# A graph layer on one core: adjacency tiles loaded one by one, or in pairs

## The reference

```python
h = jnp.maximum(_layernorm(x, axis=-1), 0.0)          # x: 10000 x 128
# _L0_gnn_ref(user_feat=h, item_feat, adj, ...)
h = item_feat @ W_item.T + b_item                      # 10000 x 128
b = user_feat @ W_user.T + b_user                      # 10000 x 128
return jax.nn.relu(adj @ h + b)                        # adj: 10000 x 10000, fp32
# result
x = x + ...
```

## Time and profile before

| | |
|---|---|
| median of three runs | 1099.3 us |
| profiled execution, time / span | 1099.52 / 1097.7 us |
| PE busy | 1090.9 us, 99% of the span |
| DVE busy | 969.6 us, 88% |
| ACT busy | 758.9 us, 69% |
| DMA | 421.56 MB, 384 GB/s over the span, the DMA engines 90% busy or more in 39 of 40 slices |
| TensorE's granted clock | full speed in all 40 slices |
| tile loads, from issue to landing | median 7.8 us for 1024 KB, 6.5 us for 904 KB (last group) |

### The profile page before, as it was taken

How to read it: one execution, slowest core, us unless ns; L and a number is a source line. 1 busy time by engine, 2 the same in 40 slices (tenths; PEclk the granted TensorE clock), 3 DMA queues, 4 the chain that set the end, 5 groups by cost and what they waited for, 6 DMA issues and landing times.

```text
span 1097.7 us, 12056 instructions
## 1 busy us (share of the span) xinstructions
PE 1090.9 (99%) x4964; PEld 898.1 (82%) x4964; DVE 969.6 (88%) x620; ACT 758.9 (69%) x474; POOL 30.8 (3%) x61
## 2 busy tenths in 40 slices
PE   9999999999999999999999999999999999999998
PEld 7788788888888888888878888888788888888887
DVE  7899989999989898889898988898989888998986
ACT  6677777667777676666776666777676667677763
POOL 0000000000000000000000000000000000000000
PEclk9999999999999999999999999999999999999999
DMA  9999999999999999999999999999999999999993
GB/s 371 416 426 426 421 353 392 365 369 402 425 384 402 361 396 370 386 391 422 415 393 365 403 370 370 414 425 396 392 366 390 376 366 395 403 399 384 372 365 129
DMA packets 64599, 421.56 MB, mean 384 GB/s; under 512 B 7960, under 2 KB 8876, under 8 KB 24608
## 3 DMA queue, kind: packets, MB, share of 16 engines
q1 hardware_dynamic: 59840, 406.21, 92.7%
q0 software_dynamic: 4416, 14.45, 4.8%
q10 hardware_dynamic: 288, 0.13, 0.0%
HBM read 415.64 MB, written 5.12 MB: 383 GB/s over the span
## 4 chain that ended last, share of the span: by engine, by line
PE 97%; DMA 1%; SPq 1%; DVE 0%; issue 0%; DVEq 0%
PE acc L608 31%; PE acc L615 31%; PE acc L609 31%; PE acc L580 2%; PE acc L549 1%; DMA items<-in_item_t 1%; PE acc L590 0%; SPq L231 0%; SPq L259 0%; SPq L258 0%; SPq L255 0%; DVE y L481 0%; PE acc L572 0%; PE acc L566 0%; DVEq L124 0%
## 5 line engine op out<-in xcount | busy, mean ns | idle before, releaser
L391 DVE TENSOR_TENSOR lo_ring<-a_ring,hi_ring 128x2048 fp32r<-128x2048 f32 (+1 forms) x381 | 849.2, 2236 | 99.5 <-ACT hi_ring L325 98.1
L325 ACT CAST hi_ring<-a_ring 128x2048 fp32r<-128x2048 f32 (+1 forms) x381 | 713.9, 1874 | 314.5 <-PE acc L615 292.0
L608 PE MATMUL acc<-hi_ring,h_lo 128*128 128x512 f32 (+1 forms) x1560 | 611.4, 392 | 0.5 <-DVE h_lo L413 0.5
L615 PE MATMUL acc<-lo_ring,h_hi 128*128 128x512 f32 (+1 forms) x1560 | 600.5, 385 | 0.0
L609 PE MATMUL acc<-hi_ring,h_hi 128*128 128x512 f32 (+1 forms) x1560 | 599.7, 384 | 0.0
L608 PEld LDWEIGHTS acc<-hi_ring,h_lo 128*128 128x128 f32 x1560 | 293.0, 188 | 65.1 <-issue 8.6
L609 PEld LDWEIGHTS acc<-hi_ring,h_hi 128*128 128x128 f32 x1560 | 293.1, 188 | 61.6 <-issue 4.6
L615 PEld LDWEIGHTS acc<-lo_ring,h_hi 128*128 128x128 f32 x1560 | 292.8, 188 | 60.4 <-DVE lo_ring L391 1.1
L406 DVE TENSOR_TENSOR h_full<-acc,bi 128x384 f32<-128x384 f32 x26 | 14.4, 554 | 17.6 <-PE acc L549 11.0
L281 POOL DMA_DIRECT2D y<-in_x_t x20 | 10.8, 540 | 563.8 <-ACT hi_ring L325 563.8
L549 PEld LDWEIGHTS acc<-wi,items 128*128 128x128 f32 x156 | 21.8, 196 | 4.2 <-DMA items<-in_item_t 1.9
(11 more groups left out here) (31 smaller groups left out, 95.6 us busy)
## 6 DMA issues: line engine op xcount, KB each, us to landing
a_ring<-in_adj_tiles SPq DMA_DIRECT2D x312, 1024.0 KB, 7.8
a_ring<-in_adj_tiles SPq DMA_DIRECT2D x78, 904.0 KB, 6.5
rows<-in_x_slices POOLq DMA_DIRECT2D x19, 256.0 KB, 7.2
y<-in_x_t POOLq DMA_DIRECT2D x19, 256.0 KB, 6.6
items<-in_item_t SPq DMA_DIRECT2D x12, 384.0 KB, 10.8
out_t<-y POOLq DMA_DIRECT2D x16, 256.0 KB, 7.3
out_t<-y SPq DMA_DIRECT2D x3, 256.0 KB, 2.4
a_rem<-in_adj_rem SPq DMA_DIRECT2D x19, 32.0 KB, 8.0
```

The source lines that it names most:

```text
L325: nc.scalar.copy(hi_ring[:, n % S_SLOTS, cols], a_ring[:, n % A_SLOTS, cols]).then_inc(hi_written, 1)
L391: nc.vector.tensor_tensor(lo_ring[:, s, cols], a_ring[:, s, cols], hi_ring[:, r, cols], ALU.subtract).then_inc(lo_written, 1)
L608: nc.tensor.matmul(acc[k][:, 0:bank_w(g, k)], h_lo[:, c, :], hi, start=(c == 0), stop=False, skip_group_check=True)
L615: last = nc.tensor.matmul(acc[k][:, 0:bank_w(g, k)], h_hi[:, c, :], lo, start=False, stop=(c == CHUNKS - 1), skip_group_check=True)
```

## The change

From tile 8 on (the ninth), SP loads two tiles with one transfer of 2 MB, into the neighbouring raw slots s and s+1. It is issued for even n alone, when PE has done tile n-7 (`old = n + 1 - A_SLOTS`), the later of the two tiles whose slots it fills. It counts on a semaphore of the pair, and ACT waits for that before either of the two casts. Tiles 0 to 7 are loaded one by one as before.

```diff
+        pair_loaded = [sem(f"pair_loaded{s}") for s in range(A_SLOTS // 2)]
...
+            def load_pair(g, c):
+                n = g * CHUNKS + c
+                s, old, w = n % A_SLOTS, n + 1 - A_SLOTS, group_w(g)
+                sp.wait_ge(chunk_used[old % S_SLOTS], old // S_SLOTS + 1)
+                sp.dma_start(a_ring[:, s:s + 2, 0:w], adj_tiles[n:n + 2, :, 0:w].rearrange("c p u -> p c u")).then_inc(pair_loaded[s // 2], 16)
...
-                    if g > 0 or c >= A_SLOTS:
-                        load_tile(g, c)
+                    if (g > 0 or c >= A_SLOTS) and c % 2 == 0:
+                        load_pair(g, c)
...
             def tile_there(g, c):
 
                 n = g * CHUNKS + c
-                act.wait_ge(a_loaded[n % A_SLOTS], (n // A_SLOTS + 1) * 16)
+                if n < A_SLOTS:
+                    act.wait_ge(a_loaded[n], 16)
+                else:
+                    act.wait_ge(pair_loaded[n % A_SLOTS // 2], n // A_SLOTS * 16)
```

## The result

| | before | changed |
|---|---|---|
| median of five runs | 1099.3 us | 1104.54 us (1103.83 to 1106.33) |
| ratio, 95% interval | | 1.005, 1.0038 to 1.0061 |
| profiled execution, time / span | 1099.52 / 1097.7 us | 1104.54 / 1102.7 us |

What follows compares the result with a forecast made beforehand. PE's work was taken as the bound, with 6.8 us idle. The profiled 1099.5 us plus 2.6 for the startup and 0 later gave 1102.1, or 1101.9 for the median; own range 1100.7 to 1103, 8-in-10 range 1099.8 to 1106.5.

Steps and rivals of the forecast that it cites:

- The steps for tiles 9, 10, 12 and 14: Startup: PE reads these tiles' first `lo` 1.2, 1.9, 2.4 and 2.9 us later than before, waiting for the pair's neighbour.
- I take each pair to land when its odd tile lands now: Startup loads: pairs 8/9, 10/11, 12/13, 14/15 ready at 33.70, 39.24, 46.07 and 52.12 us.
- lateness is not added up: Startup tiles: each lateness is against today's times, so PE's startup cost is 2.9 us less 0.3, not the sum.
- the later issue costs nothing in the early stretch: Startup: issuing 2.72 us later costs nothing, since 15 us of mostly queueing lie between issue and landing.
- I put 0 for all this, with 0 to 5 as bounds: Stretches after the startup: ACT's lead covers later issue and neighbour, cost 0; bounds allow 1.5 us in each of three groups.
- PE's end 2.6 us later: Sign of being right: PE finishes the whole run 2.6 us later, the startup's cost alone.
- PE waiting after 100 us: Sign of being wrong: PE waits after 100 us, where its idle time was forecast to stay the same.
- 14.3 against 16.3: Later stretches: an even tile's `lo` ends 14.3 us after issue, PE comes for it at 16.3, so 2 us cover.
- Three things change for an even tile, none for an odd one beyond company: All paired loads: only even tiles get later issue (2.72 us) and wait for a neighbour; odd tiles keep their timing.
- The second rival: Group starts: pairs land over 12 us after issue, PE waits 1 to 1.7 us in three groups, 1105 to 1107; chance 0.14.
- The first rival: Startup: fewer, longer transfers raise the DMA rate, pairs land earlier, run not slower, 1100 to 1101.4 us; chance 0.25.
- The third rival: Whole run: reading rows 1 MB apart in turn slows DMA below the 384 GB/s needed, 1139 us at 370; chance 0.03.

Runs made afterwards that it cites:

- tiles 8 to 15 alone: Changed kernel's pair loads for tiles 8 to 15 only, every other tile loaded singly at the old times as in the kernel before; 1101.63 us, ratio 1.0022.
- later issue alone: Against the changed kernel, two single 1 MB loads at the pair's issue time, each with its own semaphore, no wait for the neighbour; 1099.29 us, ratio 1.0001 to before.
- pairs from group 1 on: Changed kernel with single loads at the old times in group 0 and pairs only from tile 78 on; 1101.07 us, ratio 1.0015 to the kernel before.
- pairs as 1 MB transfers: Changed kernel with all its waits, but each pair sent as two 1 MB transfers counting on one semaphore; 1103.50 us, ratio 1.0042 to the kernel before.
- pairs where covered: Changed kernel with pairs only at tiles 40 to 77 of group 0 and chunks 16 to 77 of later groups, single loads elsewhere; 1099.23 us, ratio 1.0.

## Why the prediction was half right

The startup came as worked out. The steps for tiles 9, 10, 12 and 14 were 1.2, 1.9, 2.4 and 2.9 us late; measured 1.3, 2.2, 2.75 and 2.7 (the pair 14/15 landed at 51.2 and not 52.1, so it brought nothing on top). Sum of the startup: 2.6 forecast, 2.5 in the profile, 2.3 to 2.5 in the medians of three kernels. That the sum fits so well is in part luck: tiles 10 and 12 were 0.3 us later than worked out, tile 14 was 0.2 less late, and the two misses nearly cancel. "I take each pair to land when its odd tile lands now" held within 0.3 us for the first three pairs. That lateness is not added up was shown with tiles 8 to 15 alone. That the later issue costs nothing in the early stretch was shown with the later issue alone.

The mis-sized term is the one for the later stretches: "I put 0 for all this, with 0 to 5 as bounds". It is 1.8 us in pairs from group 1 on, 2.5 in the profiled execution of the changed kernel, and 2.8 and 3.7 in its two medians less the startup's 2.4. So "PE's end 2.6 us later" was half of the truth, and one of my signs of being wrong, PE waiting after 100 us, is there. The mean was right: I took 10 us from issue to landing, measured 10.3, and by my own count (14.3 against 16.3) a pair could take 12 us. The spread around the mean was wrong, and the place. I looked for the worst stretch where ACT already waited for transfers, chunks 14 to 17 of group 2, and found 1.2 us of cover; the pair 170/171 there landed 11.6 us after its issue and PE did not wait. The loss came first at chunk 6, where before no engine waited for a transfer at all: there SP issues the pair of chunks 6 and 7 just before the four stores, and it landed 12.7 us after its issue in group 1 and 13.0 in group 2. The step that failed is "Three things change for an even tile, none for an odd one beyond company": the odd tile lands later too. Against the landings of the odd tiles 85, 163 and 319 before, and with PE's lateness taken off, the pairs came 4.8, 3.1 and 4.8 us later, more than the 2.45 that I allowed, and PE lost 0.5, 0.8 and 0.7 us. The second rival named the place ("at the start of a group, when output, x and left-over items go beside the tiles") and 12 us and more, and had 0.14. Its price, 1 to 1.7 us in each of three groups, was too high for groups 1 (0.5) and 4 (0.7) and right for group 2 (1.2, with chunk 10).

The first rival asked for a landing of the pair 14/15 before 51.7, and that came: its casts begin at 51.24. I had named this as a sign of being wrong, and it does not tell the two apart. With the wait for the neighbour alone, where every load is a single 1 MB transfer at its old time, the casts of tiles 14 and 15 begin at 50.73, so longer transfers are not what brought it; what did is not shown. The rival's cause is refuted: the rate in 32:60 was 414 GB/s, not above 417. The rule of the Trainium skill on size ("DMA: Bandwidth & Descriptors", "Bandwidth") gave no gain here either: in 60:100 loads of 2 MB in a row moved 421 GB/s, loads of 1 MB in a row 426 before. The third rival is refuted as well: with rows 1 MB apart read in turn the DMA engines moved 421 GB/s in 60:100. The rule of the Trainium skill ("DMA: Bandwidth & Descriptors", "Latency and other measured facts") on rows a large power of two apart does not show at this pattern, two rows of one partition 1 MB apart: pairs as 1 MB transfers, without such a step inside a transfer, moved 422.

## What to carry to other kernels

A transfer that fills two buffers makes the first as late as the second, and since it can be issued only when both are free, the second comes later than it did by itself. Where loads already queue behind each other at full rate, it buys nothing for that. Within the startup, where the transfers come at the pace of the DMA engines, the lateness of the bound engine was the worst tile's and not the sum, so four uncovered pairs cost as much as 35. Later, where each load is issued when the bound engine frees a slot, every further wait came on top of the last (2.5, 3.0, 4.2, 5.0 us). Look for the thinnest cover where other traffic starts in a burst, and not only where an engine already waits: a place without any wait in the trace before can be the first to break.

## What the runs showed of the hardware that I had not expected

Near the edge of cover the time scatters. Later issue alone and pairs where covered stay within 0.8 us over 11 runs each, and 78 of the 80 executions of the kernel before within 1.0 us; pairs from group 1 on spread over 3.5 us in 11 runs and the changed kernel over 3.3 in 10, at a full granted clock in each profiled execution of theirs.

In the one execution where PE's gap near 27 us was 1.85 us, the granted clock of the next 5 us was 0.67; with the 1.48 us gap of the kernel before, and the 1.64 of the changed kernel's second profiled execution, it stayed at 1.00. The dip put PE 2.0 us behind at tile 6, far more than the 0.4 by which the gap had grown, and yet cost only about 0.3 us in the end, since PE waited for `lo` a few tiles later in any case.
